# A graph network layer in which the order of work in the first three and the last two steps is changed

## The reference

```python
h = relu(layernorm(x))
q, k, v = h @ Wq.T + bq, h @ Wk.T + bk, h @ Wv.T + bv
w = adj * exp(q @ k.T)
x = x + (w / w.sum(axis=2, keepdims=True)) @ v
h = relu(layernorm(x))
A = adj + eye;  d = A.sum(axis=-1) ** -0.5
L = A * d[:, None] * d[None, :]
out = x + L @ (h @ W + b)
```

## Time and profile before

| | us |
|---|---|
| median of 3 runs | 1633.65 |
| lowest, highest | 1633.39, 1633.67 |
| the profiled execution | 1633.5 |
| its span, first to last instruction | 1631.7 |
| TensorE busy | 1622.8 |
| VectorE busy | 1346.4 |
| ScalarE busy | 1075.2 |
| GpSimd busy | 802.1 |

### The profile page before, as it was taken

The page is one execution under the profiler, slowest core; times in us unless marked ns, Lnnn a source line. Parts: engine busy times, 40 slices in busy tenths (PEclk is TensorE's granted clock), DMA queues, the critical chain, the costliest instruction groups (busy, mean ns, idle before and its releaser), DMA issues.

```text
span 1631.7 us, 37843 instructions
## 1 busy us (share of the span) xinstructions
PE 1622.8 (99%) x12061; PEld 1544.9 (95%) x12061; DVE 1346.4 (83%) x3370; ACT 1075.2 (66%) x2450; POOL 802.1 (49%) x970
## 2 busy tenths in 40 slices
PE   9999999999999999999999999999999999999999
PEld 7899999999999999999999999999999999999998
DVE  6888888888888888888888888888888888888886
ACT  5676666666766766766766667667667667666663
POOL 3545544544554455455445445544554554454452
PEclk9999999999999999999999999999999999999999
DMA  5455455455455464464554554554644545545531
GB/s 184 115 128 153 124 124 151 116 134 150 109 144 133 109 159 126 117 156 122 124 151 117 133 150 109 143 133 109 158 125 118 154 124 124 151 118 133 146 89 49
DMA packets 494559, 212.66 MB, mean 130 GB/s; under 512 B 402512, under 2 KB 427344, under 8 KB 494544
## 3 DMA queue, kind: packets, MB, share of 16 engines
q1 hardware_dynamic: 492624, 210.89, 50.2%
q10 hardware_dynamic: 1920, 1.58, 0.3%
HBM read 146.28 MB, written 66.13 MB: 130 GB/s over the span
## 4 chain that ended last, share of the span: by engine, by line
PE 95%; DVE 3%; SPq 1%; issue 1%; ACT 0%; DMA 0%; POOL 0%; POOLq 0%; DVEq 0%; ACTq 0%
PE ps L982 32%; PE ps L984 31%; PE ps L985 31%; SPq L180 1%; DMA adj_blocks<-in_adj_dram 0%; DVE ht_lo L779 0%; DVE wt_lo L664 0%; DVE unused_a L941 0%; DVE g_lo L675 0%; DVE m_lo L626 0%; DVE w_lo L669 0%; DVE z_lo L762 0%; DVE wt L651 0%; SPq L210 0%; DVE late L795 0%
## 5 line engine op out<-in xcount | busy, mean ns | idle before, releaser
L454 ACT ACTIVATE g_hi<-ps,u_col 128x256 fp32r<-128x256 f32 x256 | 106.0, 465 | 310.0 <-PE ps L985 310.0
L309 POOL TENSOR_TENSOR xb<-xb,bv_row 128x512 f32<-128x512 f32 x128 | 163.5, 1299 | 275.1 <-DVE late L768 271.9
L982 PE MATMUL ps<-ht_hi,m_hi 128*128 128x256 f32 x1024 | 287.0, 280 | 2.0 <-DVE ht_lo L779 1.8
L984 PE MATMUL ps<-ht_lo,m_hi 128*128 128x256 f32 x1024 | 286.6, 280 | 0.0
L985 PE MATMUL ps<-ht_hi,m_lo 128*128 128x256 f32 x1024 | 286.3, 280 | 0.0
L982 PE MATMUL ps<-w_hi,z_hi 128*128 128x512 f32 (+1 forms) x516 | 203.1, 394 | 0.7 <-DVE z_lo L762 0.7
L985 PE MATMUL ps<-w_hi,z_lo 128*128 128x512 f32 (+1 forms) x516 | 202.8, 393 | 0.0
L984 PE MATMUL ps<-w_lo,z_hi 128*128 128x512 f32 (+1 forms) x516 | 202.5, 392 | 0.0
L982 PEld LDWEIGHTS ps<-ht_hi,m_hi 128*128 128x128 f32 x1024 | 193.2, 189 | 2.4 <-issue 2.0
L985 PEld LDWEIGHTS ps<-ht_hi,m_lo 128*128 128x128 f32 x1024 | 193.2, 189 | 0.0
L984 PEld LDWEIGHTS ps<-ht_lo,m_hi 128*128 128x128 f32 x1024 | 193.2, 189 | 0.0
(11 more groups left out here) (165 smaller groups left out, 5507.0 us busy)
## 6 DMA issues: line engine op xcount, KB each, us to landing
x_in<-in_x_dram SPq DMA_DIRECT2D x64, 512.0 KB, 5.1
xb<-in_x_dram SPq DMA_DIRECT2D x64, 512.0 KB, 4.5
out_dram<-late SPq DMA_DIRECT2D x127, 256.0 KB, 2.1
h_scratch<-h SPq DMA_DIRECT2D x62, 512.0 KB, 2.8
h_blocks<-h_scratch SPq DMA_DIRECT2D x248, 128.0 KB, 3.9
adj_in<-in_adj_dram SPq DMA_DIRECT2D x64, 256.0 KB, 3.0
adj_blocks<-in_adj_dram SPq DMA_DIRECT2D x256, 64.0 KB, 2.5
dn_row<-dn_scratch SPq DMA_DIRECT2D x64, 128.0 KB, 2.9
```

What stands on the lines that cost most here:

```text
L309: last = pool.tensor_tensor(xb[:, t, :], xb[:, t, :], bv_row[:], ALU.add)
L454: last = act.activation(g_hi[:, m, :], ps[:, G + j, m % 2 * N:m % 2 * N + N], ACT.Identity, bias=u_col[:, m:m + 1])
L982: pe.matmul(dst, a_hi[:, c, cols], b_hi[:, c, :], start=(first and c == 0), stop=False, skip_group_check=not first)
L984: pe.matmul(dst, a_hi[:, c, cols], b_lo[:, c, :], start=False, stop=False, skip_group_check=not first)
```

## The change

On ACT's queue the first quarter of Wq goes ahead of the bias columns. The warm-up has 9 matmuls instead of 17. The first half of Wv's transposes stands ahead of h^T's on TensorE, and their copies ahead of h^T's and of the turned adjacency on VectorE. ACT makes ht_sum_hi ahead of Wv's second half.

In step 2 p1 is kept ahead of h1, p5 between its two tiles; v_u2 and half of w_lo are made ahead of h1_lo; the sums and squares of x come behind z_hi; ht_lo of graph 3 comes straight behind h^T, and x1 of graph 2 with its statistics follows it, ahead of y of graph 1. The row sums of L of graph 2 move from step 2 to step 3. V6 waits for the first half of the low sums only, and V7 for the second (in every step). GpSimd's sums of h^T for graph 3 wait for ht_lo.

Step 3 is written out (third=True) with its own order: on ACT h1 with p1 and p5 first, then keep_adjacency and g_hi; on VectorE the row sums of L, h1_lo, x1b, then the turned adjacency and g_lo; on SP the next adjacency's load behind h's blocks and x's loads; dn is turned behind h. The loop starts at 4.

In step 64 the scores stand ahead of Z of graph 63, and both first results behind O; O's second tile goes to banks 0 and 1 (O_LAST). ACT's z_hi and VectorE's z_lo go behind p_hi and p_lo. In step 65 the 14 unused matmuls and the wait for y ahead of them go; y of graph 63 is made between h1_lo's two tiles and behind them, and the row sums of L of graph 64, with x1b, behind z_lo.

The diff, cut to its core:

```diff
@@ -115,7 +115,7 @@
...
-        O = (6, 2)
+        O, O_LAST = (6, 2), (6, 0)
@@ -195,7 +195,8 @@
...
-    with eng.Fori(3, B - 1) as this:
+    step(3, prev=True, main=True, ahead=True, third=True)
+    with eng.Fori(4, B - 1) as this:
@@ -221,13 +222,18 @@
...
+    def load_adj(this):
+        adj_next = adj_flat[bass.ds(sp.snap(this * (N * N)), N * N)]
+        sp.wait_ge(rsum_ready, this)
+        sp.dma_start(adj_in[:], adj_next.rearrange("(t p n) -> p t n", p=P, n=N)).then_inc(adj_loaded, 16)
@@ -242,10 +248,8 @@
...
-        if main and ahead:
-            adj_next = adj_flat[bass.ds(sp.snap(this * (N * N)), N * N)]
-            sp.wait_ge(rsum_ready, this)
-            sp.dma_start(adj_in[:], adj_next.rearrange("(t p n) -> p t n", p=P, n=N)).then_inc(adj_loaded, 16)
+        if main and ahead and not third:
+            load_adj(this)
@@ -255,6 +259,8 @@
...
+        if third:
+            load_adj(this)
@@ -268,7 +274,7 @@
...
-            load_blocks(sp, adj_next)
+            load_blocks(sp, adj_flat[bass.ds(sp.snap(this * (N * N)), N * N)])
@@ -297,6 +303,10 @@
...
+    def x1_power(graph):
+        pool.wait_ge(ve_1_done, graph)
+        pool.tensor_tensor(rs_1[:], ve_1[:], minus_half[:], ALU.pow).then_inc(rs_1_done, 1)
@@ -348,19 +358,23 @@
...
-                ht_sums_low(this)
+                ht_sums_low_half(this, 0)
+                if third:
+                    x1_power(this - 1)
+                    pool.wait_ge(ln_1_ready, this - 1)
+                ht_sums_low_half(this, 1)
...
-        if prev and main:
-            pool.wait_ge(ve_1_done, this - 1)
-            pool.tensor_tensor(rs_1[:], ve_1[:], minus_half[:], ALU.pow).then_inc(rs_1_done, 1)
+        if prev and main and not third:
+            x1_power(this - 1)
...
+            pool.wait_ge(ln_1_ready, this - 1)
@@ -370,6 +384,8 @@
...
+            if third:
+                pool.wait_ge(sd_ready, this - 1)
@@ -393,6 +409,8 @@
...
+            if prev and not older:
+                pool.wait_ge(ht_lo_ready[1], this + 1)
@@ -401,11 +419,12 @@
...
+    act.dma_start(wq_in[:, 0, :], wq[0:P, :]).then_inc(wqk_loaded[0], 16)
...
-    for o in range(DC):
+    for o in range(1, DC):
@@ -497,7 +516,7 @@
@@ -505,16 +524,19 @@
...
-            keep_adjacency(this, True)
+            if not third:
+                keep_adjacency(this, True)
...
-        if main and (not prev or older):
+        if main and (not prev or older) and not third:
...
+            if main and not older:
+                keep_p1(this)
@@ -522,26 +544,32 @@
...
-                    keep_p1(this)
+                    keep_p5(this)
+                if third:
+                    (keep_p1 if t == 0 else keep_p5)(this)
+            if third:
+                keep_adjacency(this, True)
+                g_high(0, this)
...
-            if not prev or older:
+            if (not prev or older) and not third:
...
-                keep_p5(this)
...
-            if not prev or older:
+            if (not prev or older) and not third:
...
-            elif second:
+            elif second and older:
...
+                x_sums(this + 2)
+                x_squares(this + 2)
@@ -555,17 +583,17 @@
...
+            ht_sums_high(this + 1)
...
-            ht_sums_high(this + 1)
...
-        if prev and older:
+        if prev and older and (ahead or not main):
...
-            if second and prev:
+            if second and prev and older:
@@ -575,6 +603,8 @@
...
+        if main and not ahead:
+            z_high(this - 1)
@@ -788,11 +818,24 @@
...
-    def keep_x1(t, graph):
+    def sums_of_l(graph, prev):
+        dve.wait_ge(dn_row_loaded, graph * 16)
+        if prev:
+            dve.wait_ge(x1b_ready[1], graph - 1)
+        for t in range(NT):
+            last = dve.tensor_tensor_reduce(
+                out=unused_a[:, t, :], in0=adj_kept[:, t, :], in1=dn_row[:], scale=1.0,
+                scalar=dn[:, t:t + 1], op0=ALU.mult, op1=ALU.add, accum_out=s_sum[:, t:t + 1])
+        last.then_inc(s_sum_ready, 1)
+        dve.wait_ge(s_sum_ready, graph)
+        dve.tensor_tensor(sd[:], s_sum[:], dn[:], ALU.mult).then_inc(sd_ready, 1)
+    def keep_x1(t, graph, banks=O):
+        bank = banks[t]
...
-        dve.reciprocal(rinv[:, t:t + 1], ps[:, O[t], HD:HD + 1]).then_inc(rinv_ready[t], 1)
+        dve.reciprocal(rinv[:, t:t + 1], ps[:, bank, HD:HD + 1]).then_inc(rinv_ready[t], 1)
...
-        dve.scalar_tensor_tensor(halves(x1[:, t, :]), ps[:, O[t]:O[t] + 2, 0:HD], rinv[:, t:t + 1],
+        dve.scalar_tensor_tensor(halves(x1[:, t, :]), ps[:, bank:bank + 2, 0:HD], rinv[:, t:t + 1],
@@ -820,32 +863,32 @@
...
-            keep_x1(0, this - 1)
+            keep_x1(0, this - 1, O_LAST)
...
-            keep_x1(1, this - 1)
+            keep_x1(1, this - 1, O_LAST)
...
+            dve.wait_ge(stored, (this - 3) * (16 * NT))
+            result(0, this - 2, d)
+            h1_low(1, this - 1)
...
-            h1_low(1, this - 1)
...
-            dve.wait_ge(sd_ready, this - 1)
-            add_bias(0, this - 1)
-            add_bias(1, this - 1)
...
-            dve.wait_ge(xb_ready, this - 1)
-            for t in range(NT):
-                keep_x1(t, this - 1)
-                last = x1_stats(t, this - 1)
-                if not older:
-                    (x_variance if t == 0 else x_shift)(this + 1)
-            last.then_inc(bn_1_done, 1)
+            if not third:
+                dve.wait_ge(xb_ready, this - 1)
+                for t in range(NT):
+                    keep_x1(t, this - 1)
+                    last = x1_stats(t, this - 1)
+                    if not older:
+                        (x_variance if t == 0 else x_shift)(this + 1)
+                last.then_inc(bn_1_done, 1)
@@ -856,21 +899,30 @@
...
-            transpose_adjacency(this, prev)
+            if not third:
+                transpose_adjacency(this, prev)
...
-            if older:
+            if third:
+                sums_of_l(this - 1, True)
+            elif older:
...
-            h1_low(0, this - 1)
-            add_bias(0, this - 1)
...
+                w_low(slice(0, 2))
+            h1_low(0, this - 1)
+            if third:
+                dve.wait_ge(sd_ready, this - 1)
+            add_bias(0, this - 1)
...
+            if third:
+                transpose_adjacency(this, prev)
+                g_low(0, this)
@@ -885,25 +937,26 @@
...
-            w_low(slice(0, 2))
...
+        if third:
+            turn_dn(this, prev)
...
-            transpose_adjacency(this + 1, False)
-            turn_dn(this + 1, False)
+            for c in range(2):
+                dve.wait_ge(wvt_done, c + 1)
+                dve.tensor_copy(wt[:, B11:B11 + 2, c, 0:HD], halves(ps[:, WV_BANKS[c], :])).then_inc(wvt_kept[0], 1)
...
-            for c in range(2):
-                dve.wait_ge(wvt_done, c + 1)
-                dve.tensor_copy(wt[:, B11:B11 + 2, c, 0:HD], halves(ps[:, WV_BANKS[c], :])).then_inc(wvt_kept[0], 1)
+            transpose_adjacency(this + 1, False)
+            turn_dn(this + 1, False)
@@ -913,8 +966,13 @@
...
-        if prev and older:
+        if prev and older and (ahead or not main):
...
+        if prev and not main:
+            sums_of_l(this - 1, True)
+            dve.wait_ge(sd_ready, this - 1)
+            add_bias(0, this - 1)
+            add_bias(1, this - 1)
@@ -929,23 +987,22 @@
...
-                x_shift(this + 2)
+                ht_low(this + 1, None)
+        if main and not ahead:
+            z_low(this - 1)
...
-        if main:
-            dve.wait_ge(dn_row_loaded, this * 16)
-            if prev:
-                dve.wait_ge(x1b_ready[1], this - 1)
+        if main and ahead and (not prev or older):
+            sums_of_l(this, prev)
+        if main and ahead and prev and older:
+            ht_low(this + 1, None)
+        if main and prev and not older:
+            x_shift(this + 2)
+            dve.wait_ge(xb_ready, this)
...
-                last = dve.tensor_tensor_reduce(
-                    out=unused_a[:, t, :], in0=adj_kept[:, t, :], in1=dn_row[:], scale=1.0,
-                    scalar=dn[:, t:t + 1], op0=ALU.mult, op1=ALU.add, accum_out=s_sum[:, t:t + 1])
-            last.then_inc(s_sum_ready, 1)
-            dve.wait_ge(s_sum_ready, this)
-            dve.tensor_tensor(sd[:], s_sum[:], dn[:], ALU.mult).then_inc(sd_ready, 1)
-        if main and ahead and prev:
-            ht_low(this + 1, None)
+                keep_x1(t, this)
+                last = x1_stats(t, this)
+            last.then_inc(bn_1_done, 1)
@@ -954,12 +1011,11 @@
...
-        if prev and main:
+        if prev and main and ahead:
...
-            if ahead:
-                result(1, this - 1, d)
+            result(1, this - 1, d)
@@ -989,7 +1045,7 @@
...
-        for k in range(17):
+        for k in range(9):
@@ -1056,7 +1112,7 @@
...
-        pe.wait_ge(ht_sum_lo_ready, 2 * this)
+        pe.wait_ge(ht_sum_lo_ready, 2 * this - 1)
@@ -1069,6 +1125,7 @@
...
```

(48 more changed lines are left out.)

10 lines of the change are left out of this document (5 added, 5 removed).

## The result

| | us |
|---|---|
| before, median (lowest to highest), same chip | 1633.72 (1633.32 to 1634.71) |
| after, median (lowest to highest) | 1630.88 (1629.88 to 1632.76) |
| ratio, 95% interval | 0.9982 [0.9977, 0.9988] |
| forecast | 1629.9, range 1626.0 to 1632.4 |
| profiled execution after; its span | 1629.88; 1628.0 |

What follows compares the result with a forecast made beforehand. TensorE, busy for 99% of the span, was taken to bound the kernel. 1.65 us (3.35 less 1.7 for the clock, start included) plus 2.05 at the end made 3.7 off 1633.65: 1629.9 us, range 1626.0 to 1632.4.

Steps and rivals of the forecast that it cites:

- The first graph: Start of the kernel: reordered loads and transposes bring G of graph 1 to about 25.5 us, gaining 1.45 us (1.0 to 2.0).
- The warm-up: TensorE's start: passes of 0.18 us from the first on, so 18 of them take 3.2 us and end at 4.3.
- The pause of 1.1 us: First graph, weight product on TensorE: it pauses about 1.1 us for Wq's second quarter, landing at about 9.0 us.
- Step 2: Waits of 1.0 and 0.4 us go, a new 0.9 us wait for h1_lo comes; p_lo at 67.9, O(2) doesn't wait.
- Step 3: ht_lo at 70.4 us, norm 77.2, v_u2 83.7; V7 waits 3.2 us yet comes 3.35 us sooner than before.
- The clock behind the wait: Step 3, behind V7's new wait: the long idle time drops the clock again, costing 1.7 us (1.0 to 3.4).
- What bounds step 3: Step 3: v_u2 of graph 3, ready at 83.7 us, is late next; TensorE reaches V7 at 80.5.
- The end: Last two steps: results behind O(64) and filler removed start the last z 2.05 us sooner; the z_lo wait stays.
- the first graph gives nothing: Rival for the start: ACT's chain to p_lo(1) is bound by x and GpSimd; 1631.4 us, chance 0.13.
- The rival of the clock at the start: First graph: half the warm-up doesn't hold the clock over the pause near 8 us, costing 1.7 us; 1630.4, chance 0.05.
- no new wait in step 3: Rival for step 3: ACT and VectorE keep up, so 3.2 and 1.7 us come back; 1625.0 us, chance 0.12.
- the wait grows: Rival for step 3: x1's power comes 2.4 us later and a second slow stretch follows; 1634.05 us, chance 0.08.

Runs made afterwards that it cites:

- first_only: Kernel before with only the first graph's part: Wq's first quarter ahead of the bias columns, 9 warm-up matmuls, Wv's transposes and copies ahead of hT's; 1633.90 us, ratio 0.9999.
- x_early: Changed kernel with VectorE making x's mean and variance between the quarters' bias parts instead of behind all of them; 1629.69 us, ratio 0.9976.
- no_warm: Changed kernel without any warm-up matmul; 1631.19 us, ratio 0.9984.
- x_early_fill: Changed kernel with x's mean and variance between the bias parts and 28 unused matmuls ahead of V7 in step 3; 1628.70 us, ratio 0.9968.
- wq_back: Changed kernel with the bias columns again ahead of all of Wq, still 9 warm-up matmuls; 1631.85 us, ratio 0.9990.
- e1_u2_early: Changed kernel with v_u2 in step 3 made directly behind the row sums of L; 1630.21 us, ratio 0.9977.
- u2_pool_later: x_early with step 3's v_u2 straight behind sd, and the second half of GpSimd's low sums behind sd; 1629.50 us, ratio 0.9976.
- e2_fill: Changed kernel with 28 matmuls that nothing reads ahead of V7 in step 3; 1630.23 us, ratio 0.9977.
- third_late_bias: Changed kernel, step 3 on VectorE: v_u2 between the row sums of L and sd, both bias additions and the turning of h behind z_lo; 1632.58 us, ratio 0.9992.
- third_balanced: x_early with step 3's v_u2 early, bias late, h's turning and ht_lo behind p_lo, x's power ahead of GpSimd's sums; 1631.45 us, ratio 0.9988.
- tail_only: Kernel before with only the last two steps' part: both first results behind O(64), the 14 unused matmuls out; 1631.53 us, ratio 0.9987.

## Why the prediction was nearly right, point by point

**The first graph: right in its mechanism, wrong in its sum.** Forecast: G at 25.5, 1.45 us won. The profiled execution has 25.17, but by the medians of first_only the part is worth nothing. The step that failed is "the second quarter still has both bias columns and a quarter ahead of it, and I leave its landing where it was", together with "h hangs on the load of x and the norm, which the change doesn't touch". Counting places in the queue was right, but I asked only for the quarter. The columns themselves moved back by one place and came at 7.92 (after), 8.24 and 9.34 instead of 5.79; VectorE's bias parts hang on them, and the mean of x stands behind those parts. x_early shows it from the other side: out of that order the mean is early with columns as late, and 1.2 us return. That is the size of the forecast's missing microsecond, and the profiles show no other place where it could lie than the first 130 us; but only one of the 22 executions of after has a trace, so for the median this is inferred. The spread fits too: the columns' operation (bb_out) came from 7.9 to 9.7 and the second quarter's wait was 0.2 to 2.1 us in the profiles of kernels whose first graph is the change's. Why the columns land so unevenly behind the same transfers stays open.

**The warm-up: one statement was false.** I wrote that "the warm-up passes took 0.18 us from the first on". They didn't. In windows of one microsecond the kernel before had 4, 7, 7 and 6 of them under way between 1 and 5 us, and 10 and 11 in the next two; two of these windows (PE busy, clock, DMA):

```profile
4.00:5.00 1.00, 1.00 (x6) 1.00 0.95 256
...
6.00:7.00 1.00, 1.00 (x11) 1.00 1.06 410
```

The passes start 0.21 us apart up to 5.3 us and 0.11 us apart from 5.4 us on: half clock, 1.2 GHz, and then 2.4. After, all 18 are slow ones, 4.0 / 18 = 0.22 us each; my 0.18 was the mean of slow ones and quick ones. The clock column reads 1.00 throughout, which is what misled me. It is made from a record of the granted clock that has no entry ahead of 5.38 us in the trace before, 5.12 after and 9.21 in no_warm, just where the passes become quick in each. So the 18 passes took 4.0 us, not 3.2, and the product's first pair began at 5.06, not 4.4. It cost nothing, since the second quarter came at 8.9 anyway. The Trainium skill (TensorE: Matmul & The Clock Gate, Part 1) has the throttled state as the default that activity releases: the trace agrees, and no_warm shows it plainly (passes of 512 columns 0.85 us apart at first, 0.43 later). I should have believed that sentence rather than a clock column that begins at 1.00. The pause of 1.1 us that I expected near 8 us was 0.25 after. Where it grew to 2.0 or 3.0 (x_early_fill, wq_back) the clock fell, as that rival said; where it was 2.1 (e1_u2_early) the clock stayed at 1.00, so the length of the pause alone does not decide it.

**Step 2: right.** Both old waits went and the new one for h1_lo was 0.8 (forecast 0.9). p_lo(2) ended at 68.1 (67.9), O(2) didn't wait.

**Step 3: right within 0.5 us at each station.** ht_lo at 70.7 (forecast 70.4), norm at 77.5 (77.2), v_u2 at 84.1 (83.7), V7 at 84.20 (83.7) after a wait of 3.5 (3.2). One part of the chain I had not priced: the row sums of L and sd, between the norm and h1_lo. They took 3.1 us beside GpSimd, 1.1 in u2_pool_later without it. It mattered by half a microsecond at most, because g_low(0) stands ahead of v_u2 and ACT's first half of g_high was there only near 82.5 (81.7 plus half of 1.55); g_low began at 82.98, straight behind VectorE's own work, where I had it at 82.4.

**The clock behind the wait: term a little too large.** Forecast 1.7, measured 1.2 by e2_fill and 1.4 by x_early_fill, counted from G of graph 3. The slow stretch began at 83.6 us and TensorE waited until 84.20, so that part of it fell into the wait, as the prediction allowed.

**What bounds step 3** I named as one late operation, v_u2. The runs show more than that: four other orders (e1_u2_early, u2_pool_later, third_late_bias, third_balanced) moved the wait to z_lo, p_lo or step 4's v_p, and only taking the clock's fall away gained. In the first two VectorE was busy for 9.9 of the 10 us from 80 to 90 us. In third_late_bias it was itself held up by GpSimd's power for x (2.1 us), and in third_balanced its late norm held ACT (3.7 us). That VectorE has too much work in steps 2 and 3 fits all four but isn't shown: less work wasn't tried.

**The end: right.** 2.2 us by tail_only, against 2.05.

**The sum by medians** is then 0 for the first graph, 2.2 for the end and about 0.6 for steps 2 and 3 (the remainder): 2.8. The forecast had 1.45, 2.05 and, with the first graph's share taken out, 0.2. The 0.6 is not to be leaned on: from G of graph 1 to G of graph 5 before takes 101.00 us, after 100.81, and first_only, with the old orders of steps 2 and 3, 100.81 too. By the traces, then, the new orders of these steps moved the waits and gained next to nothing. One term was 1.45 too large, and two were too small, by 0.15 and 0.4; in part it was luck that the forecast missed by no more than 1.0. Of the rivals "the first graph gives nothing" (1631.4) says what happened, yet by another cause than it gave: not x or GpSimd held p_lo(1), but the columns held h. The rival of the clock at the start (1630.4) is as near in number, but the clock did not fall there after. Neither "no new wait in step 3" nor "the wait grows" happened.

## What to carry to other kernels

When a load is moved to the front of a queue, follow what it passes as closely as the load itself: small transfers slip by a full place, and what hangs on them may stand ahead of something urgent in an engine's order. When a wait goes and one of the same size appears further on, and the engine waited for is 99% busy in between, suspect the amount of its work before trying another order: here four orders only moved the wait. And look at the spread, since a profiled execution at the fast end of it shows a gain that the median doesn't have.
